# Attention kernel: the second half's turned maxima and the values' projection moved beside the other projections, and the split of the maxima moved to VectorE

## What is computed

```python
q = (x @ Wq).reshape(B, N, H, Dh).transpose(0, 2, 1, 3)
kv = x @ Wkv
k = kv[..., :H * Dh] ...            # the same split into heads
v = kv[..., H * Dh:] ...
s = jnp.einsum('bhid,bhjd->bhij', q * scale, k)
gm = jax.lax.stop_gradient(jnp.max(s, axis=-1, keepdims=True))
p = jnp.where(causal_mask, 0.0, jnp.exp(s - gm))
num = jnp.einsum('bhij,bhjd->bhid', p, v)
out = num / (jnp.sum(p, axis=-1, keepdims=True) + EPS)
return out.transpose(0, 2, 1, 3).reshape(B, N, H * Dh) @ Wo + bo
```

## Time and profile before

| what | us |
|---|---|
| median of 3 runs | 1768.82 (1766.98 to 1769.47) |
| profiled execution, whole | 1769.09 |
| profiled execution, span | 1767.4 |
| TensorE busy in the span | 1692.5 (96%) |
| VectorE busy | 1330.6 (75%) |
| GpSimd busy | 1312.8 (74%) |
| ScalarE busy | 1066.2 (60%) |

### The profile page before, as it was taken

One profiled execution on the slowest core, in us unless ns is written; L12 is line 12 of the kernel. 1 busy time (PEld: TensorE's weight loads), 2 busy tenths in 40 slices (PEclk: granted clock), 3 DMA queues, 4 the chain that ended last, 5 costly groups with the idle time before them and its releaser, 6 DMA issues. The chain is left out here.

```text
span 1767.4 us, 35542 instructions
## 1 busy us (share of the span) xinstructions
PE 1692.5 (96%) x13182; PEld 1223.8 (69%) x13182; DVE 1330.6 (75%) x2397; ACT 1066.2 (60%) x2239; POOL 1312.8 (74%) x1354
## 2 busy tenths in 40 slices
PE   6999999999999999999999999997999878889998
PEld 4767676776767767677676776765888745568886
DVE  7777677676776776777677776756999858979887
ACT  3555545455555555546554465454989877558876
POOL 1778777677786777867777777787899866738998
PEclk9999999999999999999999999998999989989999
DMA  3000000000000000000000000010000000000000
GB/s 97 2 1 1 1 1 2 1 1 2 1 2 1 1 1 1 1 1 1 1 1 2 1 1 1 2 49 9 1 1 1 1 1 1 1 1 7 13 13 19
DMA packets 15148, 11.06 MB, mean 6 GB/s; under 512 B 481, under 2 KB 14594, under 8 KB 14978
## 3 DMA queue, kind: packets, MB, share of 16 engines
q1 hardware_dynamic: 14978, 8.80, 1.8%
HBM read 6.70 MB, written 2.10 MB: 5 GB/s over the span
## 5 line engine op out<-in xcount | busy, mean ns | idle before, releaser
L1207 DVE TENSOR_REDUCE attn_neg<-attn_shared 128x2 f32<-128x1024 f32 x512 | 611.8, 1223 | 236.2 <-PE attn_shared L1390 234.8
L1052 ACT ACTIVATE attn_prob<-attn_shared 128x1024 f32<-128x1024 f32 x288 | 295.4, 1027 | 360.6 <-PE attn_shared L1417 360.4
L948 POOL TENSOR_TENSOR attn_row_sum<-attn_row_sum,attn_prob 128x1024 f32<-128x1024 f32 (+3 forms) x256 | 418.6, 1635 | 24.5 <-POOL attn_row_sum L948 0.4
L312 ACT ACTIVATE experts_weighed<-experts_y,kept_gate 128x128 f32<-128x128 f32 x1024 | 279.4, 411 | 47.2 <-PE experts_y L559 39.4
L925 POOL TENSOR_TENSOR attn_prob<-attn_prob,attn_below 128x256 f32<-128x256 f32 x256 | 190.1, 742 | 158.4 <-ACT attn_prob L1052 158.3
L405 DVE SCALAR_TENSOR_TENSOR experts_acc<-experts_y,kept_gate,experts_acc 128x128 f32<-128x128 f32 x896 | 247.1, 342 | 22.5 <-PE experts_y L559 20.4
L1386 PE MATMUL attn_shared<-attn_qk_hi 64*128 64x512 f32 x1024 | 228.1, 428 | 8.4 <-DVE attn_neg L1207 2.2
L557 PE MATMUL experts_y<-kept_w_hi,kept_xT_hi 128*128 128x512 f32 x512 | 205.2, 401 | 3.8 <-PEq L726 1.8
L943 POOL TENSOR_TENSOR attn_row_sum<-attn_prob 128x1024 f32<-128x1024 f32 x64 | 135.8, 2122 | 97.4 <-ACT attn_prob L1052 94.9
L558 PE MATMUL experts_y<-kept_w_lo,kept_xT_hi 128*128 128x512 f32 x512 | 201.0, 393 | 0.0
L559 PE MATMUL experts_y<-kept_w_hi,kept_xT_lo 128*128 128x512 f32 x512 | 200.8, 392 | 0.0
(11 more groups left out here) (279 smaller groups left out, 3587.5 us busy)
## 6 DMA issues: line engine op xcount, KB each, us to landing
kept_x<-in_L_attn_a_x_dram SPq DMA_DIRECT2D x4, 512.0 KB, 8.7
kept_half_raw<-_ffn_expert_weights_dram SPq DMA_DIRECT2D x4, 512.0 KB, 4.8
out_dram<-kept_x SPq DMA_DIRECT2D x8, 256.0 KB, 2.3
attn_prob<-in_L_attn_a_Wkv_dram SPq DMA_DIRECT2D x2, 512.0 KB, 6.3
attn_prob<-in_L_attn_a_Wq_dram SPq DMA_DIRECT2D x1, 512.0 KB, 4.9
attn_wo<-in_L_attn_a_Wo_dram SPq DMA_DIRECT2D x4, 128.0 KB, 4.9
attn_bo<-in_L_attn_a_bo_dram SPq DMA_DIRECT2D x1, 64.0 KB, 6.0
linear_weights_raw<-in_L_attn_b_Wg_dram SPq DMA_DIRECT2D x1, 64.0 KB
```

Source lines behind the costliest of these rows:

```text
L312: ins = act.activation(weighed[n][:, e, :], y[fill(pair, quad, odd) % RING][:, e * D:(e + 1) * D], ACT.Copy, scale=k.gate[:, c, quad * PER ...
L948: pool.tensor_tensor(row_sums(p, n)[:, :, at:], row_sums(p, n)[:, :, at:], src, ALU.add).then_inc(add_ok, 1)
L1052: act.activation(prob[n % RING][:, :, :], buffer((p, t))[:, :, :], ACT.Exp).then_inc(exp_ok, 1)
L1207: dve.tensor_reduce(neg[p % 2][:, :, b, half], buffer((p, b, half))[:, :, :], AX.X, ALU.max, negate=True).then_inc(max_ok, 1)
```

## The change

It moves four kinds of work and adds none.

1. The turned maxima of the second half (`turned(p, 1)`) and ScalarE's `rows(p, 1)` move from the middle of round `p` to the end of round `p - 1`, behind the projections.
2. Both units of `values` move from the middle of a round (in round -1, from both steps) to the end, behind `project` and `outwards`.
3. What stays in the middle of a round on TensorE is products 8 to 11, the sums and products 0 to 2, with the sums now between the two groups of products. ScalarE copies the products' bank before it takes out the sums.
4. `cut` moves from GpSimd to VectorE, behind `smallest`. Of the two reciprocal pieces of a pair, VectorE makes one in step 0 and one in step 1.

The lists `shared` and `single` follow.

```diff
@@ lists of banks
-        shared += [("value", *u) for u in value_units(r, 0)]
...
-        shared += [("value", *u) for u in value_units(r, 1)]
...
+        shared += [("value", *u) for u in value_units(r)]
...
-        if valid(r):
-            single.append(("turned", r, 1))
         if valid(r + 1):
-            single.append(("turned", r + 1, 0))
+            single += [("turned", r + 1, 0), ("turned", r + 1, 1)]
@@ gpsimd
-                    if t == 0 and valid(r):
-                        cut(r, 1)
-                    if t == 1 and valid(r + 1):
-                        cut(r + 1, 0)
@@ scalar
                     if t == 0:
-                        if valid(r - 1) and r - 1 < END:
-                            denominator(r - 1, 1)
                         if valid(r - 1):
                             product_out(r - 1, 1)
-                        if valid(r):
-                            rows(r, 1)
-                        for u in value_units(r, 0):
-                            values(*u)
                         if job_at(r, 3) is not None:
                             turned_high(job_at(r, 3))
-                        if r - 1 == END:
-                            denominator(END, 1)
+                        if valid(r - 1):
+                            denominator(r - 1, 1)
...
                             high(r + 2, 0)
                             high(r + 2, 1)
+                        for u in value_units(r):
+                            values(*u)
+                        if valid(r + 1):
+                            rows(r + 1, 1)
@@ vector
+            def cut(p, n):
+
+                to = neg_cols[:, :].rearrange("p (h c) -> p h c", h=2)
+                if (p, n) == (0, 0):
+                    dve.wait_ge(zeroed, 3)
+                dve.wait_ge(least_ok, 2 * p + n + 1)
+                need(dve, turned_ok, 2 * p + n)
+                dve.tensor_copy(to[:, :, HI], least[n][:, :, :]).then_inc(cut_ok, 1)
+                dve.wait_ge(cut_ok, 2 * p + n + 1)
+                dve.tensor_tensor(to[:, :, LO], least[n][:, :, :], f(to[:, :, HI]), ALU.subtract).then_inc(neg_ok, 1)
...
                         smallest(r + 1, t)
-                    if t == 0 and valid(r - 1) or (r, t) == (END + 1, 1):
+                        cut(r + 1, t)
+                    if valid(r - 1) and r <= END:
+                        inverse(r - 1, 1, t)
+                    if r == END + 1:
                         for piece in range(PIECES):
-                            inverse(r - 1, t, piece)
+                            inverse(END, t, piece)
@@ tensor
                 row_stage(r, 0)
-                if valid(r - 1) and r - 1 < END:
-                    sums(r - 1, 1)
                 if valid(r - 1):
                     for i in range(8, 12):
                         product(r - 1, i)
-                if valid(r):
-                    turned(r, 1)
-                for u in value_units(r, 0):
-                    values(*u)
                 if job_at(r, 3) is not None:
                     turn_batch(job_at(r, 3))
                 if r == END:
                     turn_router()
-                if r - 1 == END:
-                    sums(END, 1)
+                if valid(r - 1):
+                    sums(r - 1, 1)
                 if valid(r):
                     for i in range(0, 3):
                         product(r, i)
...
                     outwards(out_group(r))
+                for u in value_units(r):
+                    values(*u)
+                if valid(r + 1):
+                    turned(r + 1, 1)
```

More of the change, by code:

```diff
@@ L1520, in _ @@
                 row_stage(r, 1)
-                for u in value_units(r, 1):
-                    values(*u)
                 if valid(r + 1):
```

15 lines of the change are left out of this document (3 added, 12 removed).

## The result

The changed kernel took 1777.5 us (median of 14 runs, 1771.9 to 1778.6), the kernel before beside it 1770.3 (14 runs, 1767.0 to 1772.0): a ratio of 1.0035, 95% interval 1.0027 to 1.0043. It is slower by 6 to 7 us; forecast was 1765.7, within 1762 to 1771. The profiled execution is one of the shorter ones, 1771.9 us with a span of 1770.1.

What follows compares the result with a forecast made beforehand. It took TensorE's stream to bound the attention stage. Terms -3.7 + 0.3 - 0.1 + 0.5 + 1.2 - 1.3 = -3.1 us gave 1766.0 from the profiled execution, 1765.7 from the median; range 1762.0 to 1771.0.

Steps and rivals of the forecast that it cites:

- The middle of the round: TensorE from products 8 to 11 to the next scores: 7.55 us before, 5.82 to 5.83 after, a gain of 1.72.
- the copy 0.1 late: In the middle, product 0 waits for ScalarE's copy of the products' bank, which comes 0.1 us late each round.
- the end: TensorE's end of a round grows by 1.56 us: projections 1.43, turned maxima 0.21, less 0.08 for a change of kind.
- the net -0.16 per round: An ordinary round: 1.56 us more at its end, 1.72 less in its middle; bounds -0.26 and +0.1.
- The minimum and the two small operations of the split by about 2.0: VectorE at a round's end: these operations are done about 2.0 us after the last score's end.
- the low halves at 6.1: VectorE at a round's end: low halves done by 6.1 us after the scores, their buffer being wanted at 7.7.
- The statistics rounds: Five rounds: maximum 0.5 us late, mostly taken up by VectorE's 0.39 idle; 0.1 charged each, 0.5 in all, bounds 0 and 2.
- The start: Round 0: ScalarE's table load comes after the second rows, first exponential 1.4 us late; cost 1.2, bounds 0 and 2.6.
- Round 30: Middle gains 0.86 us; second turned maxima wait near 1.9, hidden by GpSimd, which loses about 0.45; sum -1.3, bounds -1.5 and +0.6.
- Rival A: The waits stay hidden: ScalarE's copy is in time and the start costs nothing; -6 us, 1762.8; chance 0.24.
- Rival C: Slower: VectorE bounds the second row, its reciprocal piece waiting for later sums; 1771.5 us at 1.3 late; chance 0.17.

Runs made afterwards that it cites:

- with reductions: The changed kernel with the split of the maxima on VectorE made by four small reductions instead of a copy and a subtraction: 1769.9 us, ratio 1.0002.
- the early load: The changed kernel with a one-column exponential on ScalarE before round -2, so that the table is loaded there: 1776.2 us, ratio 1.0036.
- the splits alone: The kernel before with only the split of the maxima moved to VectorE, as copy and subtraction, in the old order: 1798.0 us, ratio 1.0162.

## Why the prediction was wrong

It said faster or the same, and the kernel is slower. By its own steps:

- **The middle of the round** (5.83; measured 5.84), the copy 0.1 late, **the end** (1.56; measured from the first projection to product 3, 432.75 to 437.20 = 4.45, against 432.77 to 435.69 = 2.92 before: 1.53) and the net -0.16 per round: right. Even rounds became 0.15 shorter each; with reductions odd ones became 0.17 shorter and batch rounds 0.00.
- **"The minimum and the two small operations of the split by about 2.0":** this is the step that failed. It took operations of 8 columns at their own size and looked at GpSimd only for what it loses, not for what it holds. On VectorE they ended at 290.2 - 287.7 = 2.5 us after the last maximum, not 0.5 to 0.7 after it. It placed the low halves at 6.1 after the scores and compared them only with the buffer wanted at 7.7; the values' projection of odd rounds, which wants the buffer of the first one, was left out. By the prediction's own times that omission alone would have cost nothing: in round 11 the projection is wanted 474.62 - 468.20 = 6.4 after the scores, and the first low halves would have been done by about 4.9 (3.7 and half of the 2.4). They were done at 474.79 - 468.20 = 6.6, since the split was 1.8 late. Price 4.9 us over the 14 rounds with output, shown by the reductions; without the reciprocal piece ahead, the same lateness would not have reached the projection.
- **The statistics rounds,** charged 0.1 each: measured +0.16 against before instead of -0.06, so 1.1 us for the five, and 0.46 in round 0's second row, where I had charged nothing. The second row loses 0.3 of the 0.5 by which the prediction has VectorE late, so its idle 0.39 absorbs less of it than the 0.4 that was counted. It is not the port: with reductions the row is still 10.58. The statistics moved to the head of the step give it back.
- **The start** (+1.2): measured +1.24 in the first row, and the early load takes it away. Right, with its mechanism: the row grew by the load's own length and no more, and TensorE's one wait for an exponential is 1.0.
- **Round 30** (wait 1.9, hidden by GpSimd, -1.3 in all): the wait was 3.6, half of it by the port (it is 1.8 with reductions, where the round still takes 34.0). It was not hidden: GpSimd itself waited 1.0 and 1.9 behind its last adds of that round for ScalarE, so it is not the bound there; and the granted clock fell behind the wait, which the prediction put at nothing. Measured +1.8 from round 30 to the experts against -1.3.
- Sum of the misses: 4.9 + 1.1 + 0.4 (round 0) + 3.1 = 9.5, less 0.3 by which round 0 began earlier, is 9.2, against 9.0 between forecast and trace.
- **Rival A's sum:** its start "costs nothing", but it takes off 0.6 where the forecast has 1.2; it should read 1762.2, not 1762.8. Nothing rests on it.
- **Rival C** (VectorE becomes the bound of the second row) was the right direction and the wrong place. After the change VectorE still idles 1.1 us ahead of ordinary second rows, as forecast; C's mechanism shows in full with the reciprocals in one step, and with the splits alone. The range left the result out because its upper end was C's alone, without the misses that come beside it.

What stays open: behind the experts' first matmul two executions of the same kernel differ by 4.4 us, and the granted clock differs with them. No run here sets where the clock comes back, and so 2 or 3 us of the ratio of a single version can't be told from it. Nor was it tried whether holding goes the other way here, VectorE holding GpSimd; the operations that could do it are 0.17 us long.

## What to carry to other kernels

When work moves to VectorE beside a busy GpSimd, ask for each operation whether it is of a kind that GpSimd holds, however small it is: its price is then the rest of GpSimd's running operation, and a reduction may do the same for 0.17 us. Follow a chain that gets longer to every consumer of its buffers in each kind of round, not to the nearest one alone. And where a wait would leave TensorE with nothing, reckon with a slower clock behind it as well: here it came behind the wait of 3.6 us and behind nine of 15 waits of 2.7 us, and cost 1.2 us or more each time.

## What the runs showed of the hardware

Copies and subtractions of 128 x 8 between SBUF tiles on VectorE took 0.17 us where they fell between two GpSimd operations, and up to 1.6 and 0.67 where one was running, in the old order up to 2.33 and 2.29, ending with it; small reductions, reciprocals of 128 x 256 and operations with one operand in PSUM kept their lengths. After a wait of 2.7 and one of 3.6 us in an otherwise full stream, TensorE's granted clock was 0.66 and 0.70 over the next 5 us, which added 1.7 and 1.2 us to work of 3.15; after six other waits of 2.7 us it stayed at 1.00.
